# Last layer of a two-layer token tower: GpSimd makes the normalised rows, VectorE no longer does

## The reference, cut to what matters

```
def _layernorm(x, axis=-1, eps=1e-05):
    m = jnp.mean(x, axis=axis, keepdims=True)
    v = jnp.var(x, axis=axis, keepdims=True)
    return (x - m) / jnp.sqrt(v + eps)

h = _L0_tok_ref(x, mask, tok_w, pos_w, type_w, gamma, beta)
h = h + _L0_attn_ref(_layernorm(h), ...)
h = h + _L0_ffn_ref(_layernorm(h), ...)     # 8 experts, the best 2 of each token
h = h + _L1_attn_ref(_layernorm(h), ...)    # 12 heads, relative positions
h = h + _L1_ffn_ref(_layernorm(h), ...)     # binary tree of 21 nodes
```

## Time and profile before

| | |
|---|---|
| three runs | 1679.48, 1685.01, 1685.82 us |
| the profiled execution | 1686.15 us, of which 1683.8 us are the span from first to last instruction |
| granted PE clock, mean of the span | 0.964 |
| busy share PE, PEld, DVE, ACT, POOL | 93, 85, 76, 67, 48 % |
| DMA | 302.35 MB, 180 GB/s mean |

### The profile page before, as it was taken

One profiled execution on the slowest core, in us unless ns is written; L12 is line 12 of the kernel. 1 busy time (PEld: TensorE's weight loads), 2 busy tenths in 40 slices (PEclk: granted clock), 3 DMA queues, 4 the chain that ended last, 5 costly groups with the idle time before them and its releaser, 6 DMA issues. The chain is left out here.

```text
span 1683.8 us, 58821 instructions
## 1 busy us (share of the span) xinstructions
PE 1570.8 (93%) x18950; PEld 1432.7 (85%) x18950; DVE 1286.3 (76%) x2845; ACT 1123.6 (67%) x3086; POOL 804.9 (48%) x1457
## 2 busy tenths in 40 slices
PE   4999999998379999999999999689999999999987
PEld 4888888886369999999999999578888888888873
DVE  5999999997875555555555555279999999999976
ACT  3999999996273333334333333278999999999961
POOL 5667777772013222222322322356777777777610
PEclk9999999999699999999999999789999999999976
DMA  3322222222117888888889989266766666666634
GB/s 94 105 73 71 71 71 71 72 72 56 56 33 215 251 264 257 252 259 258 254 259 247 265 255 250 73 217 215 240 227 231 228 222 227 234 228 229 230 102 150
DMA packets 217555, 302.35 MB, mean 180 GB/s; under 512 B 41597, under 2 KB 182610, under 8 KB 217490
## 3 DMA queue, kind: packets, MB, share of 16 engines
q1 hardware_dynamic: 200226, 263.01, 50.6%
q0 software_dynamic: 16032, 37.51, 8.4%
q10 hardware_dynamic: 1232, 1.00, 0.2%
HBM read 208.27 MB, written 93.15 MB: 179 GB/s over the span
## 5 line engine op out<-in xcount | busy, mean ns | idle before, releaser
L1092 ACT ACTIVATE prob<-ps_s,b1s 128x256 f32<-128x256 f32 x426 | 178.9, 472 | 344.6 <-PE ps_s L1059 306.2
L987 POOL DMA_INDIRECT xs<-zn_d,idx x71 | 68.9, 970 | 365.4 <-PE ps_t L1023 363.8
L1059 PE MATMUL ps_s<-xhi,w1hi_c 128*128 128x256 f32 x852 | 235.6, 295 | 1.6 <-ACT xhi L1085 1.6
L1059 PE MATMUL ps_s<-xhi,w1lo_c 128*128 128x256 f32 x852 | 226.5, 284 | 0.0
L1034 PE MATMUL ps_v<-probT,prob 128*128 128x192 f32 x852 | 208.3, 326 | 0.0
L1034 PE MATMUL ps_k<-probT,prob 128*128 128x192 f32 x852 | 208.1, 326 | 0.0
L417 PE MATMUL ps_q<-xT,wqk_c 128*128 128x128 f32 x1536 | 201.5, 283 | 2.6 <-ACT xT L659 2.2
L417 PEld LDWEIGHTS ps_q<-xT,wqk_c 128*128 128x128 f32 x1536 | 192.0, 198 | 7.0 <-ACT xT L659 3.1
L640 ACT ACTIVATE kT<-ps_q,halves 128x128 f32<-128x128 f32 (+1 forms) x512 | 172.2, 364 | 3.3
L1059 PEld LDWEIGHTS ps_s<-xhi,w1hi_c 128*128 128x128 f32 x852 | 164.0, 192 | 2.0 <-ACT xhi L1085 2.0
L1059 PEld LDWEIGHTS ps_s<-xhi,w1lo_c 128*128 128x128 f32 x852 | 164.0, 192 | 0.0
(11 more groups left out here) (233 smaller groups left out, 4147.7 us busy)
## 6 DMA issues: line engine op xcount, KB each, us to landing
rel_d<-rpad SPq DMA_DIRECT2D x64, 864.0 KB
relb<-rel_d SPq DMA_DIRECT2D x64, 768.0 KB
probT<-w2h SPq DMA_DIRECT2D x71, 576.0 KB
score<-w1h SPq DMA_DIRECT2D x71, 384.0 KB
score<-w1h SPq DMA_DIRECT2D x142, 192.0 KB
ys_d<-ys SPq DMA_DIRECT2D x71, 192.0 KB
tok<-b2h SPq DMA_DIRECT2D x71, 96.0 KB
posb<-base_d SPq DMA_DIRECT2D x128, 48.0 KB, 2.7
```

The lines of the kernel that those rows point to most:

```text
L987: pool.indirect_dma_start(xs[b][:, s, :], None, zn_d, bass.IndirectOffsetOnAxis(ap=ix[b][:], axis=0)).then_inc(x_ld[b], 16)
L1059: last = pe.matmul(dst, w, x, start=(k == 0), stop=(k == len(terms) - 1))
L1092: last = act.activation(hT[b][:, c, :], ps_s[:, j, (c % 2) * BLK:(c % 2) * BLK + BLK], ACT.Gelu, bias=b1s[b][:, c:c + 1])
```

## The change

In layer 1, `rsqrt` for the new tile gets the row of `hres` and makes `xn` on POOL: a subtraction of the mean ahead of `veps`, and a multiplication by `rs` behind `rs`. Both are 128x192 with a second operand that is one column, repeated. DVE no longer calls `normalised_rows`, and `bn_aggr` of a tile (L856 before, L870 after) now also waits until POOL has finished with the buffer `mv` two tiles back. Layer 0 is as before.

```
-            def rsqrt(t, b, var_ok, var, out_ok, out, veps=veps, deviation=None):
+            def rsqrt(t, b, var_ok, var, out_ok, out, veps=veps, deviation=None, rows=None):
                 pool.wait_ge(S[var_ok], upto(t))
+                if rows is not None:
+                    after(pool, S["xT_ps"], upto(t - 2))
+                    pool.tensor_tensor(xn[b][:].rearrange("p (o d) -> p o d", o=1), rows,
+                                       mv[b][:, 0:1].rearrange("p (o d) -> p o d", o=1).to_broadcast([128, 1, D]),
+                                       ALU.subtract).then_inc(S["pool"], 1)
+                    ch.at += 1
                 pool.tensor_tensor(veps[b][:], var[b][:, 1:2], epsc[:], ALU.add).then_inc(S["pool"], 1)
...
                 pool.tensor_tensor(out, veps[b][:], mhalf[:, 0:1], ALU.pow).then_inc(S[out_ok], 1)
+                if rows is not None:
+                    pool.wait_ge(S[out_ok], upto(t))
+                    pool.tensor_tensor(xn[b][:], xn[b][:], out.to_broadcast([128, D]), ALU.mult).then_inc(S["xn_ok"], 1)
...
                     if part == 4:
                         ch.reached(marks["e"])
                         settle(dve, spare)
+                        after(dve, S["xn_ok"], upto(te - 2))
+                        settle(dve, spare)
                         dve.bn_aggr(mv[be][:], st6[be][:]).then_inc(S["mv_ok"], 1)
...
                     add_relative()
-                    normalised_rows()
                     expert_sum(2)
```

More of the change, by code:

```diff
@@ L363, in body @@
                     rsqrt(st.tile("emb"), st.two("emb"), "mv_ok", mv, "rs_ok", rs[st.two("emb")][:],
-                          deviation=sd[st.four("emb")][:] if l == 1 else None)
-            pipeline(pool, ages, body, ch, 3 - l, behind=behind)
+                          deviation=sd[st.four("emb")][:] if l == 1 else None,
+                          rows=hres[:, bass.ds(st.tile("emb"), 1), 0:D] if l == 1 else None)
+            pipeline(pool, ages, body, ch, 3, behind=behind)
         def pe_transpose(pe, dst, src):
```

## The result

The changed kernel took 1697.83 us, the median of 4 runs (1693.87 to 1702.0), against 1682.97 us before (4 runs, 1679.48 to 1685.82): a ratio of 1.0095 [1.0073, 1.0118], so about 1% slower. The profiled execution took 1694.34 us with a span of 1692.5, 8.7 more than before.

A forecast was written before the change was run, and what follows sets the result against it. Bounds of the 8.20 us step: floors of PE (7.91) and DVE (8.04), plus waiting for gather `posb`. Two periods: +0.20 gather, -0.29 L751, +0.05 wait, +0.10 meeting = +0.06; 49 periods +1.5 us: 1688 us, range 1676 to 1708.

The forecast's parts named there:

- rival 1: POOL's `vepsz` is caught behind DVE's L742 and sustains itself: 0.28 us a period, 14 us, 1699 us; chance 0.26.
- the case that the forecast stood on: Layer 1's steady steps: a period changes by +0.03 us, 49 periods by +1.5 us, giving 1688 us; chance 0.52.
- The clock: PE's granted clock in layer 1: at the upper level, 2.4 GHz, from the second slice to the last but two.
- The operations' cost: POOL's new 128x192 subtraction and multiplication: 0.50 us of work each, between 0.34 and 0.66 us.
- The meeting of the subtraction with DVE's first operations: DVE's L839 at T+0.23 meets POOL's subtraction, reading until T+0.37: up to 0.14 us, 0.10 taken.
- The wait: DVE's added wait and register step ahead of L856: between 0 and 0.1 us a step, 0.05 taken.
- `posb` lands behind it whether it was started at T+3.7 or T+4.7: Gather `posb` lands behind the 768 KB transfer `relb`, so landing does not follow issue; +0.20 us taken.
- POOL still keeps up, with over 1 us to spare: POOL's `rsza` ends at T+6.74 instead of T+5.70, while the next L742 ends at T+8.2.
- a longer period frees `vepsz` again: Argument against capture on POOL: a longer period moves L742 back and frees `vepsz`; no size given.
- bound elsewhere: Layer 1's first ten or so steps: slower and bound elsewhere, outside the 49 steps that the change acts on.
- Rival 3: Gather `posb` follows its issue in full: +0.37 us a period, +18 us, 1704 us; chance 0.07.
- Rival 2: DVE's 0.29 us relief comes through, the period going towards PE's 7.91 us: 1671 to 1679, say 1674; chance 0.15.

The follow-up runs named there:

- experiments 9: Changed kernel with the gather one tile further ahead and `vepsz`, `rsza` ahead of the gathers in layer 1; 1679.30 us, ratio 1.0011.
- 12: Changed kernel with the gather one tile further ahead and `sd` behind the gathers, `vepsz` and `rsza`; 1677.91 us, ratio 0.9982.
- experiment 8: Changed kernel with POOL gathering one tile further ahead in layer 1; 1679.45 us, ratio 1.0004.
- Experiment 5: Changed kernel with DVE's new wait moved from ahead of L870 to L850; 1699.32 us, ratio 1.0106.
- experiments 2: Changed kernel with `sd` moved from before the gathers to behind them; 1693.58 us, ratio 1.0052.
- 3: Changed kernel with POOL's subtraction and multiplication on one column of 192, other rows left unnormalised; 1688.31 us, ratio 1.0022.
- experiment 6: Kernel before, DVE making the rows, with only `sd` moved behind the gathers, `vepsz` and `rsza`; 1674.08 us, ratio 0.9967.
- experiment 11: Changed kernel with POOL's two new operations on one column each and `sd` behind the gathers; 1676.02 us, ratio 0.9969.
- experiment 10: Changed kernel with DVE's products L850 and sums L724 in exchanged order; 1694.24 us, ratio 1.0100.
- 4: Changed kernel with DVE making the rows as before, POOL making them too into an unread buffer, DVE's new wait removed; 1700.96 us, ratio 1.0109.
- experiment 7: Kernel before with POOL gathering one tile further ahead in layer 1; 1678.39 us, ratio 1.0010.
- 1: Changed kernel with `vepsz` and `rsza` moved ahead of the gathers in layer 1; 1704.65 us, ratio 1.0124.

## Why the prediction was right and wrong

The forecast was 1688 us, no change that can be measured, and 1697.8 lies in its range and not in its case: at 0.95% the change is slower by more than the bound, and what came is for the most part rival 1, priced at 1699. The range held because it took in the rivals; the case that the forecast stood on, given 0.52, did not come. That rival 1's price lies 1 us from the median is luck in part: two errors in it nearly cancel, as said below.

- **The clock: one slice off.** The line of the earlier trace rows shows 8 tenths in layer 1's second slice (1094 to 1137 us), so the upper level is reached from the third on. Nothing in the sum hangs on it.
- **The operations' cost: right.** The subtraction takes 0.49 to 0.50 us and the multiplication 0.51, where 0.50 was taken. In steps without capture `posb` starts at T+4.8, as worked out (T+4.7). The meeting of the subtraction with DVE's first operations, priced at 0.10 us, is right too where nothing is caught: in experiments 9 and 12 the scores' sum (L738 after) starts at T+0.99 and T+1.00, in 8, where the subtraction comes after the product, at T+0.89.
- **The wait: a little more than taken,** 0.10 to 0.11 us against 0.05. Experiment 5 shows that it decides nothing.
- **"`posb` lands behind it whether it was started at T+3.7 or T+4.7": right as far as it goes.** In before and experiments 2, 3, 6 and 11 the start of `posb` varies from T+3.34 to T+4.33, and it lands 0.24 to 0.26 us behind the last packet of `relb`, 4.4 to 4.6 us behind `relb`'s start (medians). In experiment 10 it starts at T+4.81 and lands at T+7.16, earlier than before, as `relb` is early there too (T+2.41). What the step overlooked is that this cover ends. `posb` also needs 2.4 us of its own: in the changed kernel the last packet of `relb` comes at T+6.85 and `posb`, started at T+5.74, lands at T+8.15, half a microsecond later than before.
- **The step that failed is "POOL still keeps up, with over 1 us to spare", and with it the low chance of rival 1.** The sum was made for an even step of 8.20 us, and it set POOL's end against the end of L742, not against its start. By the prediction's own numbers `rsza` would start at T+5.80+0.37 = T+6.17, only 0.27 ahead of L742 at T+6.44, and before, periods went down to 7.97 us. In the step from 1207.16, of 8.03 us, L753 started at T+6.27 and `rsza` 0.01 behind it: 2.18 us instead of 0.57, and `posb` at T+5.38 in the next step. From there the capture kept itself up, in 35 of 48 steps. The argument against it, that a longer period frees `vepsz` again, is true of long steps: in those of 9.61, 8.91 and 11.11 us `vepsz` takes 0.20. But POOL is caught again at once, by `rsza`, at the end of the same step (1422 us) or of the next, of 7.9 us (1397 and 1557 us). And the steps of 8.28, with every fourth at 8.45, free nothing, since `vepsz` starts at T+6.7 to T+6.8 in them and not at T+6.55.
- **The meeting with POOL's subtraction was sized at 0.10 us, at L839.** Caught, the subtraction meets L854 instead: 0.59 us and up to 0.76 instead of 0.41. Rival 1 had this at 0.25. With L850 late by a quarter, L738 comes at T+1.40 and not T+0.88 as in experiment 8.
- **Rival 1's price: 0.28 us a period against 0.18 measured** (steps 11 to 55), and 0.07 in the steps without a miss. It had L839 at T+8.97 and the median is T+8.72. It took 3.4 us from the start of `posb` to its landing, where 2.4 are measured. What it lacked are the few steps in which the gather misses, 5.1 of 7.9 us, and 2.3 us in the first 11 steps, which I had left out as "bound elsewhere".
- **Rival 3, the gather follows its issue in full, is wrong,** as said: 2.03 us later, L850 only 0.28 later in the middle.
- **Rival 2, the relief, is there and does not come through.** Experiment 11 finds 0.11 us a step by the runs (0.18 by its profile) when nothing delays the gather. In the changed kernel the same two steps lose more than they are relieved of.

What is shown: POOL's part alone makes the loss (4), and it costs only while the gather behind it is late (8 against 7). The capture costs through that lateness, to which it adds, and not beside it (1, 9); the wait costs nothing (5). What stays open: why the first 11 steps take 6 to 7 us more than before in experiments 1, 8, 9 and 10, and less than 2 in 12; how large a share of a long step L854's hold has by itself, since it comes only where L850 is late, and experiment 10 did not separate it; and what the change would cost with the gather at T+4.8 and nothing ever caught, which no run has.

## What to carry to other kernels

An engine that is idle for a part of each step can still be on the path, through the transfers that it starts: before work is given to it, count by how much its DMA issues move, and put what nobody needs soon behind them. Moving one 0.55 us operation behind the gathers, in the kernel before, brought 0.33%; with 0.29 us taken off a full engine as well, and a small new load on POOL (experiment 11), it was no more, 0.31%. Make the sum also for the shortest steps and for every operation in the row, not only for the even step and the first of them: here one operation, 0.01 us too late, led into a state that was longer and kept itself up.

## What the runs showed of the hardware

- The lock between the two engines works in both directions. POOL's `vepsz` of 0.20 us takes 1.63 beside L753; and DVE's L854, 0.40 to 0.41 alone, takes up to 0.76 beside POOL's subtraction of two SBUF inputs. In experiment 7 the rows' operation on DVE (`xn`, one SBUF tensor input) takes 468 ns in the mean against 379 in experiment 6, so it may grow beside POOL's work too; which of POOL's operations would do it is not shown. The Trainium skill says of such a lock that issue order, not the shape, decides who blocks (SBUF — State Buffer, section "Who interferes with whom"). The traces agree where the two starts are clearly apart: in experiment 8 a product that starts 0.23 us before the subtraction keeps its 0.41 us, and in the changed kernel products that start 0.01 to 0.25 us behind it take 0.70 down to 0.47. Five that start 0.02 to 0.04 us before it by the trace are held all the same, 0.73 to 0.76.
- A POOL operation with two inputs and one of them a repeated column takes 0.49 to 0.51 us for 128x192; over the 0.18 us of one column that is 1.67 ns an element, twice the slope of one input in the earlier trace rows.
- A gather of this size lands 2.4 us after its start where the last packet of the large `relb` transfer comes 1.1 us after that start (the changed kernel) or 1.7 us (experiment 10), and 3.7 to 4.0 us after it where it is started 0.4 to 0.8 us behind `relb` (medians of before and experiments 2, 3, 6 and 11): then it lands a quarter of a microsecond behind `relb`'s last packet.
